# Slots by a maximum, a residual carried beside routed rows, a float bound in a top-k search and two moves in an attention loop, in an eight-block transformer kernel

## The reference

```python
x = x + L0_xattn(layernorm(x), ctx, ctx)
x = x + L0_ffn(layernorm(x))          # 8 experts, each takes its 128 likeliest tokens
x = x + L1_xattn(layernorm(x), ctx, ctx, mask)   # masked keys, then W_proj and b_proj
x = x + L1_ffn(layernorm(x))          # quantised activations and weights
x = x + L2_xattn(layernorm(x), ctx)   # with biases
x = x + L2_ffn(layernorm(x))          # each token goes to one of 8 experts, relu
x = x + L3_xattn(layernorm(x), ctx, ctx)         # with biases
x = x + L3_ffn(layernorm(x))          # four such steps in a row, 16 experts, silu:
# for each of the four routers: w, idx = max, argmax of softmax(xt @ router)
#     xt = w * (silu(xt @ W1[idx]) @ W2[idx])
```

## Time and profile before

| | us |
|---|---|
| median of 3 runs (lowest, highest) | 785.09 (783.3, 788.42) |
| the profiled execution | 788.19 |
| its span, first to last instruction | 786.4 |
| PE, DVE, ACT, POOL busy | 646.7, 486.2, 301.6, 202.7 |

### The profile page before, as it was taken

One profiled execution on the slowest core, in us unless ns is written; L12 is line 12 of the kernel. 1 busy time (PEld: TensorE's weight loads), 2 busy tenths in 40 slices (PEclk: granted clock), 3 DMA queues, 4 the chain that ended last, 5 costly groups with the idle time before them and its releaser, 6 DMA issues.

```text
span 786.4 us, 17704 instructions
## 1 busy us (share of the span) xinstructions
PE 646.7 (82%) x7069; PEld 393.0 (50%) x7069; DVE 486.2 (62%) x1309; ACT 301.6 (38%) x517; POOL 202.7 (26%) x276
## 2 busy tenths in 40 slices
PE   6789981699998889888977968998698698698693
PEld 3355660387455544646643535664265265265252
DVE  5557657775488678746577644655566566566561
ACT  3133330012343325244413733441374374374373
POOL 6312040212210116131027451101600600600632
PEclk9799985699899889999987989998799999799898
DMA  6910025004000000000000151000200200200202
GB/s 147 328 53 2 2 69 172 14 15 178 37 2 2 1 1 0 1 1 3 2 28 28 32 189 63 2 2 27 46 27 16 45 27 15 46 23 20 42 19 65
DMA packets 44666, 35.24 MB, mean 45 GB/s; under 512 B 12091, under 2 KB 36831, under 8 KB 44456
## 3 DMA queue, kind: packets, MB, share of 16 engines
q1 hardware_dynamic: 40440, 27.83, 11.4%
q0 software_dynamic: 2816, 5.61, 3.3%
q10 hardware_dynamic: 1328, 0.66, 0.3%
HBM read 28.09 MB, written 6.26 MB: 44 GB/s over the span
## 4 chain that ended last, share of the span: by engine, by line
PE 56%; DVE 22%; ACT 7%; issue 6%; DMA 3%; POOL 3%; another core or an unknown queue 1%; DVEq 1%; ACTq 0%; POOLq 0%; SPq 0%
PE psum L1815 6%; PE psum L577 6%; PE psum L1791 5%; PE psum L587 5%; PE psum L521 4%; PE psum L1801 3%; DVE Mp L442 3%; ACT b1r L1410 3%; PE psum L553 3%; PE psum L648 3%; ACT scr L346 2%; PE psum L782 2%; PE psum L636 2%; PE psum L622 2%; PE psum L1298 2%
## 5 line engine op out<-in xcount | busy, mean ns | idle before, releaser
L346 ACT ACTIVATE scr<-psum 128x1024 f32<-128x1024 f32 x64 | 65.6, 1025 | 106.4 <-PE psum L587 68.9
L1410 ACT ACTIVATE b1r<-big 128x512 f32 x160 | 87.5, 621 | 37.3 <-DVE be L1585 35.9
L577 PE MATMUL psum<-scr 32*128 32x256 f32 x512 | 91.3, 441 | 8.9 <-ACT scr L346 4.4
L442 DVE TENSOR_REDUCE Mp<-psum 128x8 f32<-128x1024 f32 x64 | 77.0, 1222 | 32.0 <-PE psum L577 15.0
L587 PE MATMUL psum<-Qa,scr 32*128 32x128 f32 x1024 | 94.7, 304 | 1.2 <-ACT scr L346 0.6
L521 PE MATMUL psum<-fill,identb 128*128 128x512 bf16 x295 | 80.1, 414 | 0.2
L1721 DVE COPY scr<-psum 128x512 f32<-128x512 f32 x48 | 33.2, 692 | 70.5 <-PE psum L1801 53.5
L587 PEld LDWEIGHTS psum<-Qa,scr 32*128 32x128 f32 x1024 | 69.6, 192 | 5.4 <-ACT scr L346 1.8
L322 POOL TENSOR_TENSOR scr<-KT,hmask 128x256 f32<-128x256 f32 x64 | 38.2, 614 | 121.8 <-PE psum L587 81.2
L577 PEld LDWEIGHTS psum<-scr 32*128 32x128 f32 x512 | 39.4, 189 | 42.3 <-issue 25.9
L1801 PEld LDWEIGHTS psum<-ident,scr 128*128 128x128 f32 x232 | 25.7, 147 | 56.5 <-issue 30.8
(11 more groups left out here) (392 smaller groups left out, 1278.3 us busy)
## 6 DMA issues: line engine op xcount, KB each, us to landing
big<-in_L_ffn_W SPq DMA_DIRECT2D x2, 2048.0 KB, 9.3
big<-in_L_ffn_W SPq DMA_DIRECT2D x8, 512.0 KB, 9.2
big<-in_L_ffn_W SPq DMA_DIRECT2D x1, 4096.0 KB, 13.9
y_d<-scr SPq DMA_DIRECT2D x36, 66.0 KB, 1.6
b1r<-in_L_ffn_b SPq DMA_DIRECT2D x1, 2048.0 KB, 9.7
scr<-y_d,rowi POOLq DMA_INDIRECT x36
scr<-in_ctx SPq DMA_DIRECT2D x1, 512.0 KB, 5.0
x<-in_x ACTq DMA_DIRECT2D x1, 512.0 KB, 5.7
```

The costliest lines, as they stand in the source:

```text
L346: act.activation(PT[i % 2][:, c, :], pair(WU), ACT.Exp, scale=SCALE).then_inc(S(f"exp{c}"), 1)
L442: dve.tensor_reduce(Mp[:, HC * c:HC * c + HC, DH:DH + 1], pair(2 * c).rearrange("p (j k) -> p j k", j=HC), AX.X, ALU.max, negate=True).the ...
L577: ins = pe.matmul(bank[2 * c + s // 2][:, 2 * P * n:2 * P * n + 2 * P], QT[rows, c, i, :], Km[rows, i % KB, c, :, :].rearrange("p v k -> p ...
L1410: ins = act.activation(W2d[d % len(W2d)][:, F * u:F * u + F], W2[k.layer][:, bass.ds(e * F, F)], ACT.Copy)
```

## The change

Five edits in one. (1) A row in DRAM becomes 260 numbers: values, the residual x, the token's number. In the last layer DVE forms scaled y plus residual from PSUM (`sum_output`) in place of ACT's copy, and POOL scatters it into the output; the load, the sum and the store behind it go. (2) A multiple of 4096 on the diagonal of a new matmul marks a token's own expert, so `dve_slots` takes a maximum and drops three operations; `lanes` is spread out once into `lanesx` by POOL in layer 1, and lanes are compared in two slices with the tile index innermost, `lane` in 16 bits; idle matmuls go from 25 to 18 and from 8 to 14. (3) In the search's first five rounds the lower bound is a float, and one operation follows the digit; digits alternate between banks 4 and 5. (4) In layer 1's attention the second mask product comes ahead of normalising. (5) POOL adds the output bias to x once per layer, ahead of the fifth tile's keys.

```diff
-RW = P + 4
+RW = 2 * P + 4
+OWN = 4096.0
 def pool_attention:
             for i in tiles:
+                if i == KB and L in OB:
+                    pool.wait_ge(S("ld_bo"), 16 * 5)
+                    pool.tensor_tensor(x[:, :, :], x[:, :, :], bo[:, OB[L], :].unsqueeze(1).to_broadcast([P, B, D]), ALU.add
+                                       ).then_inc(S("x_biased"), 1)
 def dve_attention:
             def residual(i):
                 dve.wait_ge(S("proj_ps"), n0 + i + 1)
+                if L in OB and i == 0:
+                    dve.wait_ge(S("x_biased"), L)
-                if L in OB:
-                    link(dve, ins)
-                    ins = dve.tensor_tensor(xi, xi, bo[:, OB[L], :], ALU.add)
...
+                if i < B and L == 1:
+                    mask_exp(i, 1)
                 if 0 < i < B:
                     normalise(i - 1)
-                if i < B and L == 1:
-                    mask_exp(i, 1)
 def dve_choice (kvm holds kv[r + 1] - 2 ** BITS[r], WHOLE = 5):
+            for r in range(WHOLE):
+                test(r, limit)
+                if r > 0:
+                    link(dve, dve.scalar_tensor_tensor(lowf[:, 0:1], digit(r - 1), -2.0 ** BITS[r - 1], lowf[:, 0:1], ALU.add, ALU.add))
+                link(dve, dve.tensor_tensor(lowf[:, 1:2], lowf[:, 0:1], kvm[:, r:r + 1], ALU.add))
+                dve.wait_ge(S("digit_ps"), r + 1)
+                link(dve, dve.tensor_tensor(cand, digit(r), lowf[:, 1:2], ALU.add))
+                limit = cand
 def pool_quantised, last:
+            pool.tensor_copy(lanesx[:, :, :], lanes[:, :].unsqueeze(2).to_broadcast([P, P, NG]))
 def dve_slots:
-            link(dve, dve.tensor_scalar(e1, totals, float(SB), 1.0 / SB, ALU.max, ALU.mult))
-            link(dve, dve.tensor_scalar(e1, e1, 0.5 + 0.5 / SB, MAGIC, ALU.subtract, ALU.add))
-            link(dve, dve.tensor_scalar(e1, e1, MAGIC, None, ALU.subtract))
-            link(dve, dve.tensor_tensor_scan(e2, ones[:, 0:E], e1, 0.0, ALU.mult, ALU.add))
-            link(dve, dve.tensor_tensor(e1, e2, e1, ALU.subtract))
-            link(dve, dve.scalar_tensor_tensor(e1, e1, float(SB), far[:, 0:E], ALU.mult, ALU.add))
-            link(dve, dve.scalar_tensor_tensor(v(lg), v(rank), float(SB), over(c1), ALU.is_ge, ALU.mult))
+            link(dve, dve.tensor_scalar(rows_more, totals, float(SB), (SB + 1) / 2, ALU.max, ALU.subtract))
+            link(dve, dve.tensor_scalar(rows_more, rows_more, MAGIC * SB, MAGIC * SB, ALU.add, ALU.subtract))
+            link(dve, dve.tensor_tensor_scan(before[:, 0:E + 1], ones[:, 0:E + 1], blocks[:, 0:E + 1], 0.0, ALU.mult, ALU.add))
+            link(dve, dve.tensor_tensor(c1[:, 0:E], before[:, 0:E], far[:, 0:E], ALU.add))
+            link(dve, dve.scalar_tensor_tensor(v(lg), v(rank), OWN + SB, over(c1), ALU.is_ge, ALU.mult))
             link(dve, dve.tensor_tensor(v(lg), v(rank), v(lg), ALU.add))
-            link(dve, dve.tensor_tensor(v(lg), v(lg), v(ohb), ALU.mult))
-            link(dve, dve.tensor_reduce(sf.unsqueeze(2), v(lg), AX.X, ALU.add))
+            link(dve, dve.tensor_reduce(sf.unsqueeze(2), v(lg), AX.X, ALU.max))
 def dve_layer:
+            def sum_output(g):
+                dve.wait_ge(S("y_ps"), chain_group(li, g) + 1)
+                dve.scalar_tensor_tensor(rows[:, g, 0:D], bank[[5, 7][g % 2]][:, 0:D], wslot[:, ORDER[g]:ORDER[g] + 1],
+                                         rows[:, g, D:2 * D], ALU.mult, ALU.add).then_inc(S("y_ready"), 1)
...
-            for b in range(0, nt, 4):
-                dve.tensor_tensor(lanen[:, b:b + 4, :], lanes[:, :].unsqueeze(1).to_broadcast([P, 4, P]),
-                                  lane[:, b:b + 4].unsqueeze(2).to_broadcast([P, 4, P]), ALU.is_equal
+            for h in range(2):
+                t = slice(nt // 2 * h, nt // 2 * (h + 1))
+                dve.tensor_tensor(lanen[:, :, t], lanesx[:, :, t], lane[:, t].unsqueeze(1).to_broadcast([P, P, nt // 2]), ALU.is_equal
                                   ).then_inc(S("lane1_ready"), 1)
...
-                if t > 2 and li < NT - 1:
-                    copy_yT(li, t - 3)
+                if t > 2:
+                    if li < NT - 1:
+                        copy_yT(li, t - 3)
+                    else:
+                        sum_output(t - 3)
 def pe_layer:
+            pe.matmul(bank[5][:, 0:E * nt], own[:, :], ohb[:, 0:E * nt], start=False, stop=False)
...
-            unread(pe, 6, 25)
+            unread(pe, 6, 18)
...
-            unread(pe, 6, 8)
+            unread(pe, 6, 14)
 @block.sync:
-            sp.dma_start(xr_d[0:B * P, 0:D].rearrange("(b p) d -> p b d", p=P), xn[:, :, :]).then_inc(S("xn_stored"), 16)
+            for n, t in enumerate((xn, x)):
+                sp.dma_start(xr_d[0:B * P, D * n:D * n + D].rearrange("(b p) d -> p b d", p=P), t[:, :, :]
+                             ).then_inc(S("xn_stored"), 16)
-            sp_combined(sp, 1)
-            for n in range(2):
-                sp.wait_ge(S("x_plus"), 3 + n + 1)
-                sp.dma_start(out[4 * n:4 * n + 4, :, :].rearrange("b p d -> p b d"), x[:, 4 * n:4 * n + 4, :]
-                             ).then_inc(S("st_out"), 16)
+            sp.wait_ge(S("rows_out"), 16 * (NG8 + NG))
 @block.gpsimd:
+            pool.memset(blocks[:, 0:1], 0.0)
+            pool.tensor_scalar(own[:, :], identb[:, :], OWN, None, ALU.mult)
-            pool.memset(padrow[:, 0:D], 0.0)
+            pool.memset(padrow[:, 0:2 * D], 0.0)
```

130 lines of the change are left out of this document (72 added, 58 removed).

## The result

Over 14 executions each, the kernel before took 788.65 (783.30 to 800.12) and the changed one 780.64 (773.81 to 783.20): a ratio of 0.990, 95% interval 0.987 to 0.993. It is faster by 8.0 us, half of the 16.7 of the sum; the forecast of 769.5 and its range (to 779) were too low. Of the 11.1 us between forecast and result 8.7 are the sum's, and 2.4 are the base: I had 786.25 from four executions. In another group of runs, where both kernels are some 35 us faster, the ratio was 0.991 (0.987 to 0.995).

The account below looks back on a forecast made before the run. No engine was taken as the bound throughout; stages take turns, with TensorE carrying 56% of the chain. The terms summed to -16.7 us, which from the four executions' average of 786.25 gave 769.5, range 760 to 779.

Parts of the forecast that it names:

- end: Kernel's end: load, sum and stores go, so it ends at the last scatter's landing plus SP's wait; -6.6 us.
- start: Before the first scores: POOL's added constants (own, a memset, 128 more padrow columns) lie on the path; +0.55 us.
- wider gathers: First gather of each of four layers: twice the bytes cost 0.2 us each, +0.8 us in all.
- last layer (ACT's relief): Last layer: ACT loses 12 scaled copies of 0.37, one standing among its weight copies on the chain; -0.6 us.
- routing: Ahead of the last four layers: fewer slot operations, faster 16-bit lane comparison; -5.0 us, only -0.1 in the relu layer.
- search: Search rounds: float bound leaves one operation after the digit in five rounds, two in the sixth; -2.15 us.
- attention: Layer 1's tiles -1.7 by the bias alone, its last product -1.6, ends of layers 1 to 3 -0.9; -4.2 us.
- lanesx copy: POOL's copy of lanesx after its quantising steps may hold up DVE's next one; +0.5 us, bounds 0 and 3.7.
- Door 1: Skill's penalty for reads leaving a 16-byte line; doubled matmuls with 24-byte weight steps would give back 0.8 us per layer.
- Rival A: Four layers' PE stretches while POOL gathers: they double with row bytes, +25 us, 794.5; chance 0.06.
- Rival B: Routing: PE's clock falls with fewer idle matmuls, +3 us in three layers, 778.5; chance 0.10.
- C: Layer 1's order stretches the loop and the search's float pair is late: together 2 us instead of 6.4, 774; chance 0.19.

## Why the prediction was wrong

The step that failed: "so the end is the landing of the last scatter and SP's wait", worth **6.6**. The stage of the load, the sum and the stores did go. But POOL's closing DRAIN, over 7.27 behind the last scatter's instruction, had been hidden under it with 0.8 to spare, and it is late next: 0.8 was gained. It stood in the trace of the kernel before, in the rows of the closing line, which no view of busy time lists; I priced the landing and never asked what every other queue still did. That is 5.8 of the 8.7 us between the sum and the 8.0 measured. The run with POOL's wait and the one without a last scatter leave no rival to it.

The second term at fault: the start, **+0.55** with bounds 0.2 to 1.0. I had priced `own` by a cast of 0.36 with nothing beside it. By itself it takes 0.54; at its place it runs beside DVE's product and takes 1.42, and the first scores come 1.24 later. The rows of before had the sign of it, in `offs` (0.82 beside that product, 0.20 behind it). With the clock, 1.3 more on average, it is +2.6, so 2.0 more; that part is a difference of means over few profiles, and its cause isn't settled.

The others, by term:

| term | forecast | measured | from |
|---|---|---|---|
| end | -6.6 | -0.8 | 9.27 to 8.47 (9.38 and 9.41 in two more profiles of before) |
| wider gathers | +0.8 | +0.7 | 2.89 to 3.13 from first gather to PE's first product, three layers; the fourth is in the next row |
| last layer (ACT's relief) | -0.6 | -0.9 | first gather to last scatter 49.48 to 48.62; 49.47 with the first edit alone, 49.09 and 50.45 in two more profiles of before, so ACT's own share isn't shown |
| routing | -5.0 | -5.2 | 3 x 1.3 (7.11 to 5.73 from first slot operation to first gather, 0.08 more ahead of it), 1.25 at li = 0 (1.55 with the end of layer 3), 0.1 in the relu layer |
| search | -2.15 | -2.14 | 16.98 to 14.84 |
| attention | -4.2 | -2.1 | layer 1: 136.05 (five profiles) to 134.30 (seven); 0.3 at the end of layer 3, nothing seen at that of layer 2 |
| start | +0.55 | +2.6 | six and eight profiles |
| lanesx copy | +0.5 | 0 to +0.57 | DVE's next step 0.75, or 1.31 to 1.33 beside the copy; in the first pair 0, else in the row of attention |
| sum | -16.7 | -7.8 | 8.0 by the medians |

The table is added up from distances in few profiles, so that its sum meets the medians to 0.2 is luck in part. The search holds to a hundredth, the routing to a quarter of a us. In the attention the mechanism was right in each part (7.44 to 7.11 a tile, 1.81 to 0.36 at the last product, and the order nothing in the loop), but over the stage, from layer 1's first exponential to layer 2's, only 1.75 of some 3.6 is there: the profiles differ by more than that in how long PE is at half clock in this stage, and which edit meets which clock isn't settled. Up to the first maximum of the quantising it is 67.6 to 65.6, 2.0 less. Behind it DVE's fourth wait for PE is 0.55 or 2.25, in profiles of both kernels, 2.25 where the half clock lies over PE's products just before. The row of 0.81 for the dropped slot operations came out as 0.81. The comparison came out at 1.9 as well, though by other parts: its two slices take 561 and 792 ns and the twelve matmuls 0.93 and not 0.78.

The copy's term was sound, and its mechanism is in the traces. In six of the fifteen profiles that have the copy it reaches into DVE's next quantising step, as here (layer 1's order back):

```profile
305.52 1.46 POOL L1296 COPY lanesx<-lanes 128x1536 bf16<-128x1536 bf16 x1
...
306.20 1.33 DVE L1216 TENSOR_SCALAR scr<-scr,qo 128x1024 f32<-128x1024 f32 x1
```

The same step takes 0.75 in the nine where the copy has ended, as in the changed kernel's first profile (copy to 305.35, step at 306.27), and 0.75 in the kernel before.

By the Trainium skill ("VectorE: DVE Perf Modes", The perf-mode tier table) the new comparison was to run at twice the old pace; 768 columns in 561 ns, against 684 for 512, is 1.8 times it, for the slice that starts before POOL's product; of those that start beside it, 768 columns take 792 and 512 took 917, 1.7 times. The rule that spoke against the edit, Door 1 of "SBUF — State Buffer", shows too, in the weight loads that step 24 bytes (count, shortest/median/longest ns), of the changed kernel:

```profile
L1955 PEld LDWEIGHTS psum<-scr x44: 138/160/168, 547.2 to 722.0; 128*128 128x128 bf16 x44
```

The loads of before, side by side in memory:

```profile
L1919 PEld LDWEIGHTS psum<-scr x44: 95/96/99, 548.3 to 727.0; 128*128 128x128 bf16 x44
```

160 ns instead of 96 each. The twelve matmuls take 0.93 instead of 0.78, so it costs 0.15 per layer at most, not the 0.8 of twelve doubled matmuls: most of the loads' time runs under the matmuls.

Rival A (wider gathers lengthen the stretches) is refuted by the spacing; the stretches exist, but depend on how closely gathers follow each other and not on bytes. Rival B: in the changed kernel's profile PE has no half clock in the routing of li = 1 to 3. B's time of 778.5 was the nearest and C's 774 nearer than mine, by luck: neither mechanism is what cost the time. Of five mechanisms not one said that the tail's replacement might already be standing behind it.

## What to carry to other kernels

When a tail is to be cut, list for each queue its own last instruction and its end, and take the second latest as the floor; a kernel whose last work is a scatter issued by POOL ends at least 8.5 us behind its issue here, and 9.8 if POOL also waits for it. Price an operation by a row of the same operation on the same engine, and look at what the other engines run at that time: here a small POOL operation with an input, beside a DVE product of two operands, lasted until that product's end or beyond (`row`, `own`, `offs`), while POOL's memsets there took no longer than elsewhere (0.09 for one column). Look also at what a longer wait ahead of PE's first work goes with in the clock. Where POOL issues many gathers into a pipeline that uses them one a tile, issue them one a tile.

## What the runs showed of the hardware that I had not expected

- POOL's closing DRAIN ends 7.26 to 7.28 us after its last indirect DMA or the wait behind it (it took 6.28 where it ran beside the work); no other engine's lasts over 2.5.
- With gathers 1.27 apart, in some groups of runs, PE's matmuls of 0.27 come 0.73 apart and its signals up to some 5 us late: about 8 us from one layer to the next in the changed kernel (58.15 against 50.22). In the three layers with gathers a tile apart it was gone, 50.8 to 51.0.
- The same chip runs the same kernel in 787 and in 752, in different groups.
- POOL and DVE side by side: 128 x 128 of 16 bits by a scalar takes POOL 0.54, and 1.42 beside DVE's product of two operands of 1152 columns; one column takes 0.18 and 1.28. The other way round, DVE's step of 1024 columns takes 0.75, and 1.31 to 1.33 when it starts beside POOL's copy.
- Wider gathers (1040 bytes a row and not 528) arrive 0.24 later, while POOL's instruction for one takes 0.96 at the median in both kernels.
